# Queries and keys in two copies of 32 partitions: the two score products of an attention step from different partitions into different PSUM banks

## What is computed

```
normed = layernorm(layernorm(t))              # 256 tokens x 192
v, gate = split(silu(normed @ W_hidden.T + b_hidden))   # 384 + 384 channels
Z = silu(normed @ W_qk.T + b_qk)              # 256 tokens x 32
q = Z * gamma[0] + beta[0]
k = Z * gamma[1] + beta[1]
A = square(relu(q @ k.T / 256))               # 256 x 256, called the scores here
out = ((A @ v) * gate) @ W_out.T + b_out
```

## Time and profile before

| what | value |
|---|---|
| three timed runs | 642.64, 643.41 and 645.22 us, median 643.41 us |
| the profiled execution: its span from the first to the last instruction | 639.0 us |
| what lies around the span, as the median less the span | 4.4 us |
| PE busy in the span | 578.6 us, 91% |
| DVE busy | 421.9 us, 66% |
| ACT busy | 334.7 us, 52% |
| POOL busy | 272.3 us, 43% |
| stages in the span | convolution to about 117 us, attention to about 323 us, experts after that |

### The profile page before, as it was taken

The page is one execution under the profiler, slowest core; times in us unless marked ns, Lnnn a source line. Parts: engine busy times, 40 slices in busy tenths (PEclk is TensorE's granted clock), DMA queues, the critical chain, the costliest instruction groups (busy, mean ns, idle before and its releaser), DMA issues.

```text
span 639.0 us, 14571 instructions
## 1 busy us (share of the span) xinstructions
PE 578.6 (91%) x3844; PEld 543.2 (85%) x3845; DVE 421.9 (66%) x1549; ACT 334.7 (52%) x722; POOL 272.3 (43%) x314
## 2 busy tenths in 40 slices
PE   3999999889989989988658999999999999999992
PEld 3899887777878877777558999999999999999992
DVE  4678888677887887888885555555555555555650
ACT  1533234555656666555256555555555555555650
POOL 3322332015645645554652444444444444444442
PEclk9899999989999999999959999999999999999998
DMA  8960000401111111111241333333333333332221
GB/s 269 409 268 0 0 2 19 149 13 56 57 37 43 68 38 37 68 43 38 69 120 32 51 50 50 50 50 50 50 51 51 51 51 50 54 39 39 39 26 19
DMA packets 31827, 42.41 MB, mean 66 GB/s; under 512 B 4597, under 2 KB 27798, under 8 KB 31671
## 3 DMA queue, kind: packets, MB, share of 16 engines
q0 software_dynamic: 13488, 13.74, 13.9%
q1 hardware_dynamic: 18196, 28.19, 13.7%
q10 hardware_dynamic: 114, 0.15, 0.1%
HBM read 24.49 MB, written 17.57 MB: 66 GB/s over the span
## 4 chain that ended last, share of the span: by engine, by line
PE 37%; DMA 6%; DVE 3%; issue 3%; POOL 1%; POOLq 0%; ACT 0%; DVEq 0%; ACTq 0%
PE ps L1268 35%; DMA out_rows<-const,y_id 6%; PE ps L1273 1%; PE ps L1272 1%; POOL y_id L675 1%; DVE we_lo L1222 0%; POOL out_rows L679 0%; POOLq L204 0%; DVE over L1087 0%; DVE n_tiles L1089 0%; DVE const L1246 0%; ACT we_hi L814 0%; DVE table_parts L1092 0%; DVE const L1252 0%; DVE table_parts L1097 0%
## 5 line engine op out<-in xcount | busy, mean ns | idle before, releaser
L823 ACT ACTIVATE hT<-ps,b_i_sb 128x256 f32<-128x256 f32 (+1 forms) x240 | 95.0, 446 | 119.9 <-PE ps L1268 119.8
L1268 PE MATMUL ps<-w_o_sb,hT 128*128 x852 | 145.3, 327 | 0.9 <-DVE const L1246 0.9
L679 POOL DMA_INDIRECT out_rows<-const,y_id x71 | 123.2, 1736 | 42.0 <-POOL y_id L675 29.4
L1268 PEld LDWEIGHTS ps<-w_o_sb,hT 128*128 128x128 f32 x852 | 137.5, 191 | 1.2 <-issue 1.2
L1268 PE MATMUL ps<-n_hi,we_hi 128*128 128x256 f32 (+1 forms) x480 | 129.8, 293 | 4.4 <-DVE n_hi L1230 2.5
L1268 PEld LDWEIGHTS ps<-n_hi,we_hi 128*128 128x128 f32 x480 | 92.5, 193 | 5.4 <-DVE we_lo L1222 4.9
L1268 PE MATMUL ps<-n_hi,we_lo 128*128 128x256 f32 (+1 forms) x480 | 96.4, 283 | 0.0
L1222 DVE TENSOR_TENSOR we_lo<-we_all,we_hi 128x768 fp32r<-128x768 f32 x80 | 73.2, 957 | 22.0 <-issue 20.7
L1268 PEld LDWEIGHTS ps<-n_hi,we_lo 128*128 128x128 f32 x480 | 74.8, 193 | 0.0
L1268 PE MATMUL ps<-nA_lo,we_hi 128*128 128x256 f32 (+1 forms) x240 | 67.8, 283 | 0.0
L1246 DVE TENSOR_TENSOR const<-ps,b_o_sb 128x384 f32<-128x384 f32 (+1 forms) x40 | 20.5, 512 | 69.7 <-PE ps L1268 37.5
(11 more groups left out here) (235 smaller groups left out, 1168.7 us busy)
## 6 DMA issues: line engine op xcount, KB each, us to landing
we_all<-in_w_i SPq DMA_DIRECT2D x8, 768.0 KB, 13.6
conv_only<-lists SPq DMA_DIRECT2D x31, 194.0 KB, 2.9
w_o_sb<-in_w_o SPq DMA_DIRECT2D x8, 576.0 KB, 17.8
out_rows<-X SPq DMA_DIRECT2D x16, 192.0 KB, 1.9
X<-in_x SPq DMA_DIRECT2D x1, 1536.0 KB, 11.3
out_rows<-const,y_id POOLq DMA_INDIRECT x71, 3.6
conv_only<-lists SPq DMA_DIRECT2D x9, 97.0 KB, 2.5
we_all<-in_w_hid SPq DMA_DIRECT2D x1, 776.0 KB, 7.1
```

The source lines that it names most:

```text
L679: pool.indirect_dma_start(out=out, out_offset=bass.IndirectOffsetOnAxis(ap=y_id[:, odd, t:t + 1], axis=0), in_=y_sb[:, odd, t, :], in_offs ...
L823: last = act.activation(hT[:, odd, f, 0:n].unsqueeze(1), ps_h[:, b, c, 0:n].unsqueeze(1), ACT.Gelu, bias=b_i_sb[:, ds(e * FCHUNKS + f, 1)])
L1268: return pe.matmul(dst, lhsT, rhs, start=start, stop=stop)
```

## The change

Queries and keys are made twice, in partitions 0 to 31 and 32 to 63. For that the weights and the bias of z are laid out twice side by side (64 columns in place of 32), and gamma and beta are loaded into both halves of their tile, by four DMAs in place of two. The product of half t of the keys reads copy t, and writes its 256 columns into bank t. Bank 0 also holds the transposed rows, so PE waits for `sim_done` of image i before it transposes the rows of image i+1. The waits on `ld_attn` count two more DMAs.

```diff
+TWIN_QK = HALVES * QK
...
-        w_qk_sb = sb("w_qk_sb", [P, 2, QK])
-        w_qk_hi = sb("w_qk_hi", [P, 2, QK], f32r)
-        w_qk_lo = sb("w_qk_lo", [P, 2, QK], f32r)
+        w_qk_sb = sb("w_qk_sb", [P, 2, TWIN_QK])
+        w_qk_hi = sb("w_qk_hi", [P, 2, TWIN_QK], f32r)
+        w_qk_lo = sb("w_qk_lo", [P, 2, TWIN_QK], f32r)
...
-        gb_sb = sb("gb_sb", [QK, 4])
+        gb_sb = sb("gb_sb", [TWIN_QK, 4])
...
-        zT, qT, kT = (xc[0:QK, :, :, :].rearrange("p a t c -> p (a t c)")[:, n * SEQ:(n + 1) * SEQ] for n in range(3))
+        zT, qT, kT = (xc[0:TWIN_QK, :, :, :].rearrange("p a t c -> p (a t c)")[:, n * SEQ:(n + 1) * SEQ] for n in range(3))
...
-        ps_z = ps[0:QK, 1, 0:SEQ]
-        ps_sim = ps[:, 1, :].rearrange("p (t n) -> p t n", t=HALVES)
+        ps_z = ps[0:TWIN_QK, 1, 0:SEQ]
+        ps_sim = ps[:, 0:2, 0:SEQ]
...
-            sp.dma_start(gb_sb[:, 0:2], gamma).then_inc(ld_attn, 16)
-            sp.dma_start(gb_sb[:, 2:4], beta).then_inc(ld_attn, 16)
+            for t in range(HALVES):
+                own = slice(t * QK, (t + 1) * QK)
+                sp.dma_start(gb_sb[own, 0:2], gamma).then_inc(ld_attn, 16)
+                sp.dma_start(gb_sb[own, 2:4], beta).then_inc(ld_attn, 16)
...
-                products(ps_z, w_qk_hi, w_qk_lo, slice(0, QK), False).then_inc(z_ps, 1)
+                products(ps_z, w_qk_hi, w_qk_lo, slice(0, TWIN_QK), False).then_inc(z_ps, 1)
...
                     for t in range(HALVES):
-                        last = mm(ps_sim[:, t, :], kT[:, t * P:(t + 1) * P], qT[:, :])
+                        own = slice(t * QK, (t + 1) * QK)
+                        last = mm(ps_sim[:, t, :], kT[own, t * P:(t + 1) * P], qT[own, :])
                     last.then_inc(sim_ps, 1)
...
                 if not absent(i + 1) and not under_conv(i + 1):
+                    pe.wait_ge(sim_done, i + 1)
                     transpose_normed(i + 1)
...
-    w_qk = np.ascontiguousarray(two_parts(L1_attn_W_qk).swapaxes(0, 1))
+    w_qk = two_parts(L1_attn_W_qk).swapaxes(0, 1)
+    w_qk = np.ascontiguousarray(np.concatenate([w_qk] * HALVES, axis=-1))
```

More of the change, by code:

```diff
@@ L347, in build @@
         b_hi = late_buffer(SLICE, KBB)
-        b_hid_sb, b_qk_sb, b_qk_hi = late_buffer(SLICE, 1), late_buffer(QK, 1), late_buffer(QK, KBB)
+        b_hid_sb, b_qk_sb, b_qk_hi = late_buffer(SLICE, 1), late_buffer(TWIN_QK, 1), late_buffer(TWIN_QK, KBB)
         w_out_t_sb = late_buffer(NKC * HID, KC).rearrange("p (k f) -> p k f", k=NKC)
@@ L383, in build @@
         ps_table = [ps[0:1, 5, 0:2 * P], ps[0:1, 7, 0:2 * P], ps[0:1, 7, 2 * P:4 * P]]
-        prep_at = np.cumsum([0, HID, QK, 2 * EXPERTS, HID // P * EXPERTS]).tolist()
+        prep_at = np.cumsum([0, HID, TWIN_QK, 2 * EXPERTS, HID // P * EXPERTS]).tolist()
         ps_b_hid, ps_b_qk = ps[0:KBB, 7, 0:HID], ps[0:KBB, 7, prep_at[1]:prep_at[2]]
@@ L661, in attn_step @@
                                 in_=rows[:, t, :], in_offset=None).then_inc(scattered, 16)
-            pool.wait_ge(ld_attn, 16 * 5)
+            pool.wait_ge(ld_attn, 16 * 7)
             pipeline(pool, attn_step, **ATTN)
@@ L1201, in attn_step @@
                     first_table()
-            dve.wait_ge(ld_attn, 16 * 5)
+            dve.wait_ge(ld_attn, 16 * 7)
             dve.wait_ge(pads_ready, 1)
@@ L1365, in _ @@
             pipeline(pe, conv_step, **CONV)
-            pe.wait_ge(ld_attn, 16 * 5)
+            pe.wait_ge(ld_attn, 16 * 7)
             pe.wait_ge(bf_set, 1)
@@ L1529 @@
         "w_hid": w_hid, "w_qk": w_qk, "b_hid": b_hid,
-        "b_qk": np.asarray(L1_attn_b_qk).reshape(1, -1), "b_i": np.ascontiguousarray(b_i.T),
+        "b_qk": np.tile(np.asarray(L1_attn_b_qk), HALVES).reshape(1, -1), "b_i": np.ascontiguousarray(b_i.T),
         "gamma": np.ascontiguousarray(np.asarray(L1_attn_gamma).T),
```

## The result

The changed kernel takes 652.75 us (median of four runs, 648.39 to 655.93), the kernel before 644.32 us in the same comparison (642.64 to 645.30): a ratio of 1.0133, with an interval of 1.0088 to 1.0178. It is slower by 1.3%; the forecast was 643.5 us and no change. Every ratio in this document is of fast runs alone; two runs are left out as slow, one of the changed kernel with the bias addition later (635.33 us) and one of the kernel before (652.08 us).

What follows compares the result with a forecast made beforehand. It took the path through POOL and DVE, not PE, to bound the attention step. Span 639.0 + 0 (scores, wait, z) + 0.1 (start) = 639.1 us, plus 4.4 from span to median: 643.5 us; range 641.0 to 646.0.

Steps and rivals of the forecast that it cites:

- The score products: Attention's two score products side by side: 0.25 us of PE saved a step, at most 0.53, worth 0 in time.
- The new wait: PE waits for Relu before the transposes: cost 0, since the wait is over at least 0.65 us before.
- z with 64 columns: Wider weight loads for queries and keys stay hidden under matmuls: 0; shown bare, 0.41 us.
- 64 partitions: ACT and DVE work on 64 partitions costs nothing more; if doubled, DVE loses at most 0.8 us.
- The start: Extra loads and wider weight and bias preparation before the attention: 0.1 us more, bounds 0 and 1.2.
- The turn: One attention step, 12.18 us between gated products, set through POOL and DVE, with DVE standing behind POOL's bias addition.
- this case as a rival: PE's clock falls behind longer waits in the attention: 5.6 us lost in 15 steps, 649 us; chance 0.04.
- Its price: Falling clock in an attention step: 1.55 us of work lost, 1.18 to spare, so 0.37 us a step.
- 1.18 us of PE's path was taken as spare: PE's path through an attention step has 1.18 us to spare beside the path through POOL.

Runs made afterwards that it cites:

- the changed kernel with the bias addition later: Changed kernel with POOL's output-bias addition moved from behind the power to just before the scatters: 629.10 us, ratio 0.9736 to the kernel before.
- both from copy 0: Changed kernel with both score products reading copy 0, so they can't run side by side: 643.26 us, ratio 1.0021 to the kernel before.
- two idle matmuls, wait cut: Changed kernel with two unread matmuls before z, held until DVE's router diff is done: 643.38 us, ratio 1.0018 to the kernel before.
- the kernel before with the addition later: Kernel before with POOL's output-bias addition moved from behind the power to just before the scatters: 628.13 us, ratio 0.9767 to the kernel before.
- two idle matmuls: Changed kernel with two matmuls whose result nobody reads put before z's products: 645.30 us, ratio 1.0028 to the kernel before.
- wait cut alone: Changed kernel with one tiny unread matmul before z, held until DVE's router diff is done: 654.83 us, ratio 1.0165 to the kernel before.

## Why the prediction was wrong

Right, by its own steps:

- **The score products:** the saving was taken as 0.25 us, at most 0.53, and is 0.42. It goes into the wait before z, as foreseen, and is worth nothing by itself, even where the steps are 11.1 us long.
- **The new wait, z with 64 columns, 64 partitions:** nothing, as priced; Relu is over 1.1 us before the transposes.
- **The start:** taken as 0.1 us. The profiled execution began the attention 3.9 us later, but two kernels with all that the change adds at the start began it at 118.77 and 118.69 us (both from copy 0; two idle matmuls, wait cut), before the 119.65 of the kernel before; and the kernel before with one gate product less, which has none of it, began at 123.23. So this spread isn't the change's. The granted clock from 0 to 40 us went with the start in part: 0.96 for 118.69 and 118.77, 0.91 for 119.65, 0.87 for 123.23 and 123.57, but 0.96 for 121.18 (the kernel before with the addition later). All four kernels with long steps began late, at 123.2 to 123.6 us, with 0.87 there; but two idle matmuls (125.13) and the changed kernel with the addition later (123.76) began as late with 0.87 and have no long step, so a late start alone doesn't bring the falls.
- **The turn** through the gated product, POOL and DVE: the moved addition shows that DVE stood behind POOL, and that this set the 12.2 us.

Wrong was one step: the score products' saving was put at 0 in the sum because a longer wait of PE before z was taken to cost nothing. The longer wait came, 1.4 us in place of 0.93, and with it the clock fell in six steps, which took 10.4 us more in the profile. The prediction had this case as a rival, at 0.04. It had the place and the direction right, and failed in two ways.

Its chance rested on comparing the length of one wait: 3.12 us, behind which the clock fell, and 0.93, behind which it didn't, and 1.2 to 1.5 called nearer to the second. The cut wait shows that this was the wrong thing to compare; cutting 1.4 us into 0.7 and 0.5 leaves six falls. And two points, far apart, say nothing of the ground between them; a forecast that moves PE into that ground should have given the rival something like even odds.

Its price was too low: 0.37 us a long step, since 1.18 us of PE's path was taken as spare. The rows above show why none was. In a long step DVE is late by 1.63 us (its addition starts 226.37 - 222.26 = 4.11 us after the output product, and 198.58 - 196.10 = 2.48 in the undisturbed step), and now meets POOL's power and addition not at L1039 (L1042 here) but at the logits before: L1151 (L1154 here) takes 1.67 us, not 0.35. The stall behind POOL is paid in every step, 1.2 us at one instruction or 1.3 at another, so lateness of PE goes through whole: 1.65 to 1.87 us. By that price six long steps make 10 us, and the timed medians, 8.4 us apart, fit a similar number.

Shown by experiments: that PE's missing work brings the falls (taken away without the change, put back with it, and twice as much with nearly twice the effect), and that the falls make the loss. They aren't peculiar to the profiled runs: all 16 timed runs of the four kernels with long steps had a mean clock of 0.944 to 0.968, and the runs of the kernel before that are counted beside the experiments 0.971 to 0.981. Only argued: how DVE's stall moves to the logits, which is read from one profile. Open: why the falls come in runs of neighbouring steps and not in all. In three profiles (changed, one gate product less, wait cut alone) the first long step is the same one, from 200.1, 199.8 and 199.9 us; with two gate products less it starts at 163.6.

The Trainium skill ("TensorE: Matmul & The Clock Gate", the table under "Why this matters for your kernels") asks both for a busy TensorE and for short gaps between bursts of matmuls. By its row on gaps alone the waits of 1.4 us would have left the clock as it was. The runs here differ from that row and decide: the clock fell with the work, and cutting the gaps didn't help.

## What to carry to other kernels

An engine that waits in each step has a second price for being faster: if TensorE has less work in a step whose length others set, its clock may fall, as it did here, and then it is late on the path where it had been just in time. Before shortening TensorE's work off the path, find what sets the step (here POOL's addition in front of DVE) and shorten that. And slack that is made of another engine's stall isn't slack until the stall is shown to go away.

## What the runs showed of the hardware that was not expected

- Taking 0.36 us a step of ordinary matmuls away from PE made a kernel 1.35% slower, and putting four idle matmuls a step into another gave the loss back (1.0133 to 1.0017).
- DVE's small instructions can be held while POOL's bias addition runs: 1.43 us for two instructions of 128x16, 1.67 for two of 128x8, 0.86 for one of 128x8. The Trainium skill ("SBUF — State Buffer", "SBUF: two separate sides") has an exclusive lock on the ports that VectorE and GpSimd share, held for a whole instruction; the trace agrees, with these instructions ending 0.03 to 0.17 us behind POOL's addition. Not every meeting holds DVE: under POOL's power, from 251.80 to 252.53 us in the kernel before with the addition later, L1052, which reads two tiles, took 0.18 us, as it does at 192.88 in the changed kernel with POOL's addition over.
